# First layer of a graph network: which operand of the aggregation is held in TensorE, and in which orientation its sums are kept

## The reference, cut to what matters

```
adj = A * (y @ y.T)                       # A: 5000 x 5000 of zeros and ones, y: one-hot labels, 16 classes
adj = adj / maximum(sum(abs(adj), axis=1), 1e-12)
support = adj @ input                     # 5000 x 5000 times 5000 x 128
x = layernorm(x + 0.9 * support + 0.1 * h0)
```

## Time and profile before

| what | value |
|---|---|
| time before, median of 3 | 6264.59 us (6263.4 to 6265.18) |
| profiled execution, its own time | 6271.09 us |
| span of its trace | 6269.3 us |
| granted TensorE clock, mean | 0.861 |
| TensorE matmuls busy | 4393.9 us (70%) |
| VectorE busy | 5090.3 us (81%) |
| ScalarE busy | 2200.1 us (35%) |
| first layer's loop and the stage behind it | from about 43 us to 581.5 us of the span |

### The profile page before, as it was taken

How to read it: one execution, slowest core, us unless ns; L and a number is a source line. 1 busy time by engine, 2 the same in 40 slices (tenths; PEclk the granted TensorE clock), 3 DMA queues, 4 the chain that set the end, 5 groups by cost and what they waited for, 6 DMA issues and landing times. The chain is left out here.

```text
span 6269.3 us, 78468 instructions
## 1 busy us (share of the span) xinstructions
PE 4393.9 (70%) x27812; PEld 3146.2 (50%) x27812; DVE 5090.3 (81%) x12501; ACT 2200.1 (35%) x3353; POOL 291.1 (5%) x170
## 2 busy tenths in 40 slices
PE   6997688888779546263588778445278888837982
PEld 2443277777669545263477677445122222217982
DVE  5887388888628888998999999993679999975865
ACT  2332477777521111111245444232232221215542
POOL 0000000000030000000000000000002022110000
PEclk9998699999899778686799888777699999968996
DMA  7552000000057323041122222102033333314840
GB/s 198 201 202 98 17 2 2 2 2 2 1 157 227 110 82 112 26 139 53 47 74 79 76 69 69 35 2 34 18 112 106 111 109 108 105 29 187 298 173 17
DMA packets 183473, 546.63 MB, mean 87 GB/s; under 512 B 24603, under 2 KB 66702, under 8 KB 182902
## 3 DMA queue, kind: packets, MB, share of 16 engines
q1 hardware_dynamic: 177846, 536.71, 26.2%
q0 software_dynamic: 5120, 3.97, 0.3%
HBM read 528.97 MB, written 11.56 MB: 86 GB/s over the span
## 5 line engine op out<-in xcount | busy, mean ns | idle before, releaser
L680 PE MATMUL ps<-ident,arena 125*125 125x125 f32 x3200 | 539.4, 302 | 1030.1 <-DVEq L1189 1030.1
L680 PEld LDWEIGHTS ps<-ident,arena 125*125 125x125 f32 x3200 | 468.5, 214 | 1071.6 <-DVEq L1189 1071.6
L1491 DVE SCALAR_TENSOR_TENSOR arena<-arena,pair 125x1000 f32<-125x1000 f32 x800 | 939.2, 1252 | 70.7 <-ACT arena L1454 70.7
L794 ACT ACTIVATE turned<-ps 125x500 f32<-125x500 f32 x800 | 465.4, 585 | 1438.5 <-PE ps L680 1438.1
L688 PE MATMUL ps<-arena,turned 125*125 125x129 f32 x6400 | 917.6, 291 | 6.0 <-ACT turned L794 6.0
L1509 PE MATMUL ps<-arena 125*64 125x500 f32 x3200 | 764.0, 601 | 193.4 <-DVE arena L1491 193.4
L688 PEld LDWEIGHTS ps<-arena,turned 125*125 125x125 f32 x6400 | 843.8, 203 | 18.2 <-ACT turned L794 12.0
L712 PE MATMUL ps<-arena 125*125 125x129 f32 x6400 | 733.4, 275 | 24.5 <-ACT arena L805 17.4
L712 PEld LDWEIGHTS ps<-arena 125*125 125x125 f32 x6400 | 718.0, 188 | 59.6 <-issue 26.7
L1509 PEld LDWEIGHTS ps<-arena 125*64 125x64 f32 x3200 | 198.0, 137 | 756.4 <-DVE arena L1491 525.2
L1139 DVE SCALAR_TENSOR_TENSOR arena<-arena,wt 125x5000 f32<-125x5000 f32 x80 | 434.1, 5427 | 110.5 <-issue 110.5
(11 more groups left out here) (349 smaller groups left out, 5840.3 us busy)
## 6 DMA issues: line engine op xcount, KB each, us to landing
arena<-in_adj_tiles SPq DMA_DIRECT2D x400, 500.0 KB, 4.5
arena<-in_adj_wide SPq DMA_DIRECT2D x400, 500.0 KB, 4.4
arena<-in_adj_wide SPq DMA_DIRECT2D x100, 1000.0 KB, 4.5
x_saved<-arena SPq DMA_DIRECT2D x2, 2240.0 KB
arena<-x_saved SPq DMA_DIRECT2D x2, 2240.0 KB
arena<-att_saved SPq DMA_DIRECT2D x1, 2257.5 KB
arena<-in_x SPq DMA_DIRECT2D x1, 2240.0 KB
arena<-in_h SPq DMA_DIRECT2D x1, 2240.0 KB
```

The lines of the kernel that those rows point to most:

```text
L680: mm = pe.transpose(banks_turn[:, g % 2, c * P:(c + 1) * P], work[b % depth][:, j:j + P], ident[0:P, 0:P])
L794: a.activation(turned[:, g % 2, :], banks_turn[:, g % 2, :], ACT.Copy)\
L1491: v.scalar_tensor_tensor(out=weight(m).rearrange("p (g w) -> p g w", g=2), in0=rows(ERB + h * N + r * PASS, PASS).rearrange("p (g w) -> p ...
```

## The change

The aggregation swaps its operands. A quad's block of 125 sources x 125 targets becomes the weights, and the 128 features of the source block are streamed, so that the sums come out node-major: 125 target nodes on the partitions, four blocks of 128 features along one PSUM bank. Each source block takes four matmuls in place of one. The four accumulations share a bank. A matmul with `start=True` opens the whole bank, so one such matmul per group comes first: zeros from one row of `cols` times one row of labels, 512 columns wide. All others have `start=False`. `keep` writes the sums where the residual wants them, `mag_sum` moves from the area VB to the area KT, which the feature-major sums have left, and the stage with the transposes is gone.

```diff
-            mag_sum = lambda s: rows(VB + (s % 2) * QW, QW)
+            mag_sum = lambda s: rows(KT + (s % 2) * QW, QW)
             gram = lambda k: ps[0:P, k, 0:GW]
-            agg, norm = lambda s: ps[0:F, 4 + s % 2, 0:GW], lambda s: ps[0:P, 6 + s % 2, 0:GC]
+            agg, norm = lambda s: ps[0:P, 4 + s % 2, 0:GC * F], lambda s: ps[0:P, 6 + s % 2, 0:GC]
+            none = cols[0:1, 256:256 + P]
...
                     if i == 0 and s >= 2:
                         pe.wait_ge(s_agg_kept, s - 1)
+                    if i == 0:
+                        pe.matmul(agg(s), none, labels(0)[0:1, 0:GC * F], start=True, stop=False)
                     for k in range(QUAD):
                         c = i * QUAD + k
-                        mm = pe.matmul(agg(s), nodes(VA, FA)[:, c, 0:F], quad(q)[:, k * GW:(k + 1) * GW],
-                                       start=(c == 0), stop=(c == NB - 1))
+                        for j in range(GC):
+                            at = k * GW + j * P
+                            mm = pe.matmul(agg(s)[:, j * F:(j + 1) * F], quad(q)[:, at:at + P],
+                                           nodes(VA, FA)[:, c, 0:F], start=False,
+                                           stop=(c == NB - 1 and j == GC - 1))
                     mm.then_inc(s_agg, 1)
...
                     a.wait_ge(s_agg, (s + 1) * PER)
-                    a.activation(rows(KT + s * GW, GW, F), agg(s), ACT.Copy).then_inc(s_agg_kept, 1)
+                    a.activation(nodes(VB, FA)[:, s * GC:(s + 1) * GC, 0:F],
+                                 agg(s).rearrange("p (c f) -> p c f", c=GC), ACT.Copy).then_inc(s_agg_kept, 1)
...
-        with nc.semaphore("l0_back") as s_back, nc.semaphore("l0_copied") as s_copied, nc.Block() as block:
-            @block.tensor
-            def _(pe):
-                for g in range(NG):
-                    if g >= 2:
-                        pe.wait_ge(s_copied, g - 1)
-                    for c in range(GC):
-                        o = (g * GC + c) * P
-                        mm = pe.transpose(ps[0:P, g % 2, c * F:(c + 1) * F], rows(KT + o, P, F), ident[:, :])
-                    mm.then_inc(s_back, 1)
-
-            @block.scalar
-            def _(a):
-                for g in range(NG):
-                    a.wait_ge(s_back, g + 1)
-                    a.activation(nodes(VB, FA)[:, g * GC:(g + 1) * GC, 0:F],
-                                 ps[0:P, g % 2, :].rearrange("p (c f) -> p c f", c=GC), ACT.Copy)\
-                     .then_inc(s_copied, 1)
```

## The result

The changed kernel takes 6289.1 us (median of 6 runs, 6286.1 to 6293.31), the kernel before 6264.68 us (6 runs, 6263.4 to 6265.9). The ratio is 1.0037, with a 95% interval of 1.0026 to 1.0048: 24.4 us slower. The forecast was 6281.5 us in a range of 6270 to 6292, and slower.

The account below looks back on a forecast made before the run. TensorE paces the first layer's loop, VectorE only 0.1 us a quad behind; 13.7 + 8.6 - 8.8 + 3.4 = +16.9 us on the profiled 6271.09, less 6.5 of profile cost, gives 6281.5 us, range 6270 to 6292.

Parts of the forecast that it names:

- The swapped aggregation: First layer's loop: 32 records a quad take 3.491 us, not 3.354; 100 quads grow by 13.7 us.
- The price from L1246: Record pace taken from L1246, which streams the same 128 columns at full clock: 0.1091 us each.
- The slower pace of L712: Rival for the aggregation: 0.1106 us a record beside a busy VectorE, +18.5 us, 6286 us; chance 0.15.
- loads in the open: Rival for the aggregation: weight load and stream follow each other, +340 us, about 6605 us; chance 0.02.
- The opening matmul: Before each group's aggregation: 512 columns in two records, 0.86 us, 10 times, 8.6 us.
- the rival with 0.08: Opening matmul hidden beside the label products, costing nothing: +8.3 us, 6273 us; chance 0.08.
- the rival with 0.05: Opening matmul pulls the clock down: ten more low stretches, +17 us, 6298 us; chance 0.05.
- The stage: Stage after the loop goes: L347 starts 0.31 us after the loop's last operation, saving 8.8 us.
- The clock at +3.4 us: Behind the sums of weights: two more double low stretches than before, 2 x 1.7 = 3.4 us.
- The bound of +7: Upper bound of the clock term behind the sums: four more double low stretches.
- The rival on the other side: Clock stays at 1.00 around the sums: ten stretches of 1.7 us go, -3.5 us, 6261 us; chance 0.05.
- The residual's start: L347, right behind L283 after the loop, was to start at 572.95 + 22.3 + 3.4 = 598.7 us.

Follow-up runs that it names:

- the pieces' experiments: Sums of weights in four pieces of four matmuls, keep two quads later, in both kernels: changed kernel 6258.43 us, kernel before 6244.31 us.
- the longer groups: Kernel before with the first matmul of each group issued three more times: 6299.24 us, ratio 1.0062.

## Why the prediction was right, and where a size was off

- TensorE paces the loop, and what it has more to do is paid in full: right. VectorE's wait grew from 66.0 to 111.0 us.
- The swapped aggregation at 13.7 us: 14.0 (98 quads), and the pieces' experiments bear the sum out. The price from L1246 was 0.1091 us a record, 0.1095 came. The slower pace of L712, a rival with 0.15, did not appear.
- By the rule that the prediction quotes from the Trainium skill, "TensorE: Matmul & The Clock Gate", section "The mechanism", load and stream don't overlap in the same row groups; it would have cost hundreds of microseconds (the rival "loads in the open"). This case's trace doesn't agree: load and stream lie side by side, at 0.1095 us a pair, where one after the other they would need about 0.21.
- The opening matmul at 8.6 us: 9.3, since the first of them runs at the low clock. It isn't hidden (the rival with 0.08) and doesn't pull the clock down (the rival with 0.05): with the sums in pieces the clock is 1.00 with the opening matmuls in place, and taking them out left seven of nine stretches long.
- The stage at -8.8 us: right, and the residual follows `keep` by 0.31 us; no wait for `keep` or `mag_sum` appears in the loop.
- **The clock at +3.4 us: mis-sized, about 10.** That it is the group's length which puts the sums at other places against the falls was right, and the pieces and the longer groups show it. The step that failed is how often the long kind comes. I took two more of them; there were eight and not one behind the nine inner sums. I worked with a group of 53.4 us and "ever other places". But that length, which came only after the one short stretch (53.32), leaves out what a long stretch itself adds: with one, the group lasts 54.89 us, the falls come 54.61 us apart, and the sums stay at the places where the stretch is long. The bound of +7 was too narrow too. That the time still fell into the range is luck for this term: the range had room left by the bounds of the others.
- The rival on the other side, a clock that stays up, didn't come, with the sums left in one piece. In the experiments with pieces the clock stayed up.
- The residual's start was forecast at 598.7 and came at 608.35: of the difference of 9.7 some 6.8 are the clock, 1.8 the loads ahead of the loop, 0.7 the opening at the low clock, and the rest the quads.
- I took the 6.5 us of the profiled execution over the median for the profile's cost. The changed kernel's profiled one is 2.3 us under its median. These two executions differ by 10.8 us in the later stages, so a profile's distance from its median isn't a fixed price.

## What to carry to other kernels

When TensorE sets the pace, price a swap of operands by the distance of records of the same form: here 32 fresh loads of 125 columns cost 3.50 us where 8 streams of 500 columns cost 3.35, and with 112 streamed columns in place of 128 beside the load the quad was only 0.02 us shorter. When falls of the clock come once a group, work out the group's length with the low stretch in it, since the stretch moves the next fall's place. Look for streaks of narrow matmuls: 3.4 us of one-column work in a row cost 1.7 to 3.4 us of clock on top, and the same work in four pieces cost none, which won 19 us in the kernel before, more than its stage with the transposes costs (8.8). A bank shared by several accumulations can be opened by the first real matmul; a separate wide one costs 0.84 us each time.

## What the runs showed of the hardware that was not expected

- How long the clock stays low behind a sum (3.41 or 6.83 us) goes with the fall's place: up to 3.75 us after the sum's start it was long and from 4.07 us on short, 36 times in four profiles. So 2.5 us more work in a group cost 3.2 us in the first layer; in the changed kernel the clock took 10 of the 24 us.
- In the one execution with 64 columns streamed beside each fresh load TensorE, its records following one another without a gap, stayed at the low level for the whole loop of 960 us, by the length of its records; with 112 and 128 it ran at the high one outside the stretches behind the sums.
- The kernel before, measured again beside these runs, spread over 6254.31 to 6269.29 us in 15 runs; a difference of some microseconds needs the trace's stage, not the total, to be read.
